# First small-head layer: the transpose that spreads the inverse row sums is issued behind the products with values, not ahead of them

## Chip, cores and metric

The kernel runs on one NeuronCore of one Trainium2 chip. The metric is the device time of one launch in microseconds, the median of three runs. All times inside the profile are from one profiled execution of the same program.

## What is computed

Four pre-norm decoder blocks over x of 8 batches x 128 positions x 256 features, each with an attention-like part, a cross part and a feed-forward part. The change touches only the attention of block 1 ("l1a" in the kernel): 32 query heads of width 8, in 8 groups that share keys and values, causal softmax.

```python
q = (x @ Wq).reshape(B, S, H, dk).transpose(0, 2, 1, 3)      # H = 32, dk = 8
k = (x @ Wk).reshape(B, S, HKV, dk).transpose(0, 2, 1, 3)    # HKV = 8
v = (x @ Wv).reshape(B, S, HKV, dk).transpose(0, 2, 1, 3)
q, k = _rope(q), _rope(k)
qg = q.reshape(B, HKV, G, S, dk)                             # G = 4
scores = jnp.einsum('bhgqd,bhkd->bhgqk', qg, k) / jnp.sqrt(jnp.float32(dk))
attn = jax.nn.softmax(scores + mask, axis=-1)
out = jnp.einsum('bhgqk,bhkd->bhgqd', attn, v)
return out.transpose(...).reshape(B, S, D) @ Wo
```

## The kernel before

Everything is float32 on 128 partitions, in one program with an instruction stream per engine that is written out by hand; semaphores order the engines. PSUM has 8 banks of 512 columns. A plan made ahead gives every job (one filling of a bank) a bank in turn, modulo 8. TensorE's `begin` waits until the bank's earlier user has been read (bank_free), and `end` puts the bank's full signal on the last instruction of the job.

The head loop of l1a works on 64 units (8 batches x 8 key groups). A unit is four heads: 128 queries x 4 x 128 keys of scores, one bank. `heads_plan` makes rounds of three units. In round r the order is: the scores of the round's three units ("s": three matmuls that write the causal mask, then three with the 32 rows of queries and keys), the products with values of a group x of four units where one has become due ("pv"), the transposes of the probabilities of the round before ("t": four 128x128 transposes a unit, twelve a round), and where due the output product of two batches ("o"). There are 16 groups, x = 0 to 15; three rounds of four have one.

The other engines follow the same plan:

- VectorE takes the maxima of each unit's scores (L2425). For pv it first works on the sums of the group (`inverse_of`: L2398, L2400, and L2404, which spreads the 16 inverse sums over 128 columns in SBUF and signals inverse_sums), then copies the unscaled values' products of group x out of the bank (L2445), then scales the outputs of group x - 1 by what the transpose has put into the second half of the same bank (`scaled_outputs`, L2410). It also copies the transposed probabilities of odd units (L2434).
- ScalarE makes the exponentials, four instructions a unit (L1733); the last one frees the bank of the scores. It copies the transposed probabilities of even units (L1739).
- GpSimd folds each unit's probabilities twice (L712, L717) toward the row sums.

So the bank of pv x holds two things: columns 0 to 127 the products of group x with the values, columns 128 to 255 the transposed spread of the inverse sums of group x - 1. The second is one 128x128 transpose, L995, whose source was ready a round before. The products of group x read the copied transposes of units 4x to 4x+3, and wait for the copies of 4x+2 and 4x+3. The inverse of the last group, 15, has a bank of its own ("rb", L1008). Group 0 has no L995.

Lines: L890 is the helper `mm` (all matmuls), L904 the transposes of a normalised input, L987 the transposes of probabilities, L995 the transpose in question.

Of the kernel before, what the change touches and what calls it, by code (L numbers as in the profile page):

```python
# [6 lines left out]
P = 128  # L7
# [237 lines left out]
def build(nc, a, out):  # L245
# [3 lines left out]
    with ExitStack() as ctx:  # L249
# [626 lines left out]
        def _(pe):  # L876
# [74 lines left out]
            def heads(layer, wo, pad):  # L951

                kbd = r3(wk(0, 8 * N), N)
                for key in heads_plan(SUMS_AT if layer == "l2x" else None):
                    if key[0] == "ws":
                        o = begin(layer, "ws")
                        pe.wait_ge(weight_sums, 3)
                        end(mm(o[:, 0:3], cst("ones"), sm(128, 3), True, True))
                        continue
                    if key[0] == "qt":  # L960
                        quantised_transposes("l2x", 0)
                        continue
                    if key[0] == "s":
                        if key[1] % 3:
                            continue
                        units = round_of(key[1] // 3)
                        if layer == "l1a" and UNITS // 2 in units:

                            pe.wait_ge(dve_to_pe.sem, dve_to_pe.next())
                            pe.wait_ge(act_to_pe.sem, act_to_pe.next())  # L970
                        os = [begin(layer, "s", u) for u in units]
                        for u, o in zip(units, os):
                            b = u // 8
                            if pad is None:
                                mm(o, identb[:, :], causalb[:, :], True, False)
                            else:
                                mm(r3(o, P), identb[:, :], pad[:, b * P:(b + 1) * P].unsqueeze(1).to_broadcast([P, 4, P]), True, False)
                        for u, o in zip(units, os):
                            r, b, c = 32 * (u % 4), u // 8, u // 4 % 2
                            end(mm(r3(o, P), XN[r:r + 32, c * N + b * P:c * N + (b + 1) * P],  # L980
                                   kbd[r:r + 32, 4 * c:4 * c + 4, b * P:(b + 1) * P], False, True), layer, "s", u)
                        continue
                    o = begin(layer, *key)
                    if key[0] == "t":
                        pe.wait_ge(*freed(J(layer, "s", key[1])))
                        for i in range(4):
                            ins = nc.tensor.transpose(o[:, i * P:(i + 1) * P],  # L987
                                                      wk(12288 + (key[1] % 8) * G + i * P, P), cst("ident"))
                        end(ins)
                    elif key[0] == "pv":  # L990

                        x = key[1]
                        if layer == "l1a" and x:
                            pe.wait_ge(inverse_sums, x)
                            nc.tensor.transpose(o[:, P:2 * P], inverse_spread(x - 1), cst("ident"))  # L995
                        pe.wait_ge(*freed(J(layer, "t", 4 * x + 2)))
                        pe.wait_ge(*freed(J(layer, "t", 4 * x + 3)))
                        for part in range(1 if layer == "l1a" else 2):
                            for h in range(4):
                                for k in range(4):  # L1000
                                    u = 4 * x + k
                                    window = v_windows[:, u * 32 + 24 - 8 * h:u * 32 + 56 - 8 * h] if part == 0 else ones_window[:, 24 - 8 * h:56 - 8 * h]
                                    ins = mm(o[32 * k:32 * k + 32, part * P:(part + 1) * P], window,
                                             wk(8192 + (u % 8) * G + h * P, P), h == 0, h == 3)
                        end(ins)
                    elif key[0] == "rb":
                        pe.wait_ge(inverse_sums, key[1] + 1)
                        end(nc.tensor.transpose(o[:, P:2 * P], inverse_spread(key[1]), cst("ident")))  # L1008
                    else:
                        bp = key[1]  # L1010
                        for x in range(4):
                            pe.wait_ge(*freed(inverse_job(4 * bp + x) if layer == "l1a" else J(layer, "pv", 4 * bp + x)))
                        for i in range(2):
                            for c in range(2):
                                lo = (bp % 2) * G + (2 * i + c) * P
                                ins = mm(o[:, i * D:(i + 1) * D], XT[:, lo:lo + P],
                                         wo[:, c * D:(c + 1) * D], c == 0, c == 1)
                        end(ins)
# [47 lines left out]
            for b in range(NB + 2):  # L1066
# [6 lines left out]
                if b >= 2:  # L1073
                    x = b - 2
# [1939 lines left out]
```

## Time and profile before

| | us |
|---|---|
| median of three runs | 1522.03 |
| lowest, highest | 1521.43, 1523.54 |
| the profiled execution | 1525.09 |
| its span | 1523.3 |
| head loop of l1a in it, about | 415 to 513 |

The page gives the busy time of each engine over the span: PE (TensorE matmul) 90%, PEld (its weight loads, beside the matmuls) 56%, DVE (VectorE) 60%, ACT (ScalarE) 50%, POOL (GpSimd) 35%. These are averages over some twelve stages with different limits, so a small edit in one stage is read in that stage: in the timeline of each engine, and in the chain of work that ended last. In a timeline row "x12" is twelve instructions merged, and the bracket at the end is the idle time of the engine before them and what the reader of the trace takes for its release. One float32 matmul as written leaves two records (x32 for sixteen), a transpose leaves one. Some matmul records are missing; "x2" for the three mask matmuls is such a place, and the weight loads (x3) show when they began.

### The profile page before, as it was taken

To read this page: it belongs to the slowest core of one execution; us is meant where nothing else is said; L and a number is where in the kernel's file an instruction comes from. 1 tells how busy PE (TensorE), PEld (TensorE's weight loads), DVE (VectorE), ACT (ScalarE), POOL (GpSimd) and SP (SyncE) were. 2 spreads that over 40 slices of the span, in tenths; PEclk is the share of its full clock that TensorE was granted. 3 is DMA by queue.
4 is the path that set the end of the run, shared out by engine and by line. 5 is a ranking of instruction groups with operands and counts; after the bars stand their busy time and mean duration, and the time that the engine had idled before them with its cause. 6 is when DMAs were issued, how large, how long until landed. Compare 5 with 4: busy or idle time off the path is not lost.

```text
span 1523.3 us, 24834 instructions
## 1 busy us (share of the span) xinstructions
PE 1372.9 (90%) x9246; PEld 855.1 (56%) x9264; DVE 919.2 (60%) x1713; ACT 767.3 (50%) x1847; POOL 528.1 (35%) x528
## 2 busy tenths in 40 slices
PE   7869999999888879999999998998996789988799
PEld 3434555565455545666667774664663545545536
DVE  7784322224588755545555788855787587686631
ACT  3452111111788567776776456457776455363230
POOL 3230000000277468886882000110843435414200
PEclk9979999999999999999999999998998798988899
DMA  8020211001200300000000100020001100000100
GB/s 257 26 86 1 68 53 41 1 0 60 107 2 2 126 0 8 8 8 8 8 8 1 77 23 1 1 83 2 2 2 72 56 1 2 3 0 3 30 0 28
DMA packets 21851, 48.06 MB, mean 32 GB/s; under 512 B 1506, under 2 KB 16995, under 8 KB 20580
## 3 DMA queue, kind: packets, MB, share of 16 engines
q1 hardware_dynamic: 21732, 46.47, 8.9%
q8 instruction: 75, 1.23, 0.3%
q14 instruction: 44, 0.36, 0.1%
HBM read 41.22 MB, written 5.24 MB: 31 GB/s over the span
## 4 chain that ended last, share of the span: by engine, by line
PE 64%; DVE 21%; ACT 6%; issue 5%; POOL 4%; DMA 0%; DVEq 0%; ACTq 0%; POOLq 0%
PE PS L890 47%; PE PS L1128 5%; DVE work L2638 4%; PE PS L1187 3%; PE PS L891 3%; ACT work L1733 2%; PE PS L987 2%; PE PS L1225 2%; DVE small L2076 2%; DVE small L2425 1%; PE PS L904 1%; DVE work L2222 1%; DVE X L2617 1%; DVE work L2606 1%; POOL work L823 1%
## 5 line engine op out<-in xcount | busy, mean ns | idle before, releaser
L890 PE MATMUL PS<-XT,WB 128*128 128x512 f32 (+1 forms) x688 | 300.8, 595 | 5.2 <-DVE XT L2102 2.9
L890 PEld LDWEIGHTS PS<-XT,WB 128*128 128x128 f32 (+1 forms) x688 | 127.1, 191 | 149.8 <-issue 146.1
L1733 ACT ACTIVATE work<-PS,small 128x128 f32<-128x128 f32 x512 | 137.7, 416 | 43.6 <-DVE small L2425 43.6
L2297 DVE TENSOR_TENSOR work<-PS,work 128x512 f32<-128x512 f32 x48 | 33.1, 691 | 170.1 <-PE PS L890 170.1
L1659 ACT ACTIVATE work<-PS 128x512 f32<-128x512 f32 x48 | 28.7, 597 | 194.6 <-PE PS L890 194.6
L2425 DVE TENSOR_REDUCE small<-PS 128x4 f32<-128x512 f32 x128 | 80.5, 684 | 36.1 <-PE PS L890 34.6
L890 PE MATMUL PS<-XT,WA 128*128 128x512 f32 (+2 forms) x224 | 97.9, 600 | 4.4 <-DVE XT L2102 2.3
L666 POOL TENSOR_SCALAR small<-small 128x4 f32<-128x4 f32 x22 | 5.1, 230 | 268.3 <-DVE small L2079 268.2
L2638 DVE SCALAR_TENSOR_TENSOR work<-PS,vec,work 128x508 f32<-128x508 f32 (+2 forms) x108 | 80.2, 743 | 13.7 <-DVE work L2638 6.5
L1128 PE MATMUL PS<-WB,work 128*128 128x256 f32 x384 | 86.9, 379 | 0.5 <-DVE work L2302 0.5
L890 PE MATMUL PS<-WA,XT 128*128 128x256 f32 (+1 forms) x384 | 81.5, 374 | 3.6 <-DVE XT L2410 1.8
L1128 PEld LDWEIGHTS PS<-WB,work 128*128 128x128 f32 x384 | 72.8, 190 | 18.3 <-issue 7.7
L890 PE MATMUL PS<-work 128*128 128x64 f32 (+4 forms) x368 | 75.4, 358 | 3.0 <-DVE work L2690 1.8
L890 PEld LDWEIGHTS PS<-WA,XT 128*128 128x128 f32 x384 | 70.7, 202 | 12.8 <-issue 5.0
L701 POOL COPY WB<-WB 128x1536 f32<-128x1536 f32 x8 | 11.7, 1468 | 186.4 <-PE PS L890 186.4
L890 PEld LDWEIGHTS PS<-XT,WA 128*128 128x128 f32 (+2 forms) x224 | 40.0, 189 | 58.2 <-issue 52.1
L1578 ACT ACTIVATE XN<-X,small 128x256 f32<-128x256 f32 x44 | 24.0, 593 | 93.0 <-DVE small L2085 92.9
L987 PE MATMUL PS<-cst,work 128*128 128x128 f32 x512 | 67.2, 281 | 2.7 <-ACT work L1733 2.7
L904 PE MATMUL PS<-cst,XN 128*128 128x128 f32 x176 | 36.0, 353 | 36.3 <-DVE XN L2089 35.5
L890 PE MATMUL PS<-WB,C 128*128 128x256 f32 (+1 forms) x287 | 67.3, 379 | 0.2
L987 PEld LDWEIGHTS PS<-cst,work 128*128 128x128 f32 x512 | 56.3, 143 | 19.4 <-issue 19.4
L1187 PE MATMUL PS<-work 128*128 128x256 f32 x256 | 65.8, 387 | 0.0
(388 smaller groups left out, 2988.3 us busy)
## 6 DMA issues: line engine op xcount, KB each, us to landing
WB<-in_l0f SPq DMA_DIRECT2D x8, 768.0 KB, 8.1
WB<-in_l1x SPq DMA_DIRECT2D x1, 6144.0 KB, 18.3
WB<-in_l0f SPq DMA_DIRECT2D x32, 96.0 KB, 7.2
WB<-in_l2f SPq DMA_DIRECT2D x1, 3072.0 KB, 10.0
WA<-in_l3a SPq DMA_DIRECT2D x1, 2624.0 KB, 9.3
WB<-in_l3f SPq DMA_DIRECT2D x1, 2064.0 KB, 7.9
WA<-in_l1f SPq DMA_DIRECT2D x1, 2056.0 KB, 11.2
C<-in_ctx SPq DMA_DIRECT2D x2, 1024.0 KB, 7.1
```

The costliest lines, as they stand in the source:

```text
L890: mm = lambda o, l, r, s, e: nc.tensor.matmul(o, l, r, start=s, stop=e)
L891: more = lambda o, l, r, e: nc.tensor.matmul(o, l, r, start=False, stop=e, skip_group_check=True)
L904: ins = nc.tensor.transpose(o[:, i * P:(i + 1) * P], source[:, b * D + c * P:b * D + (c + 1) * P], cst("ident"))
L987: ins = nc.tensor.transpose(o[:, i * P:(i + 1) * P], wk(12288 + (key[1] % 8) * G + i * P, P), cst("ident"))
L1128: ins = nc.tensor.matmul(o[:, i * D:(i + 1) * D], l0f_h(x)[:, b * P:(b + 1) * P], quad(x // 3, "down")[:, x % 3 * D:(x % 3 + 1) * D], star ...
L1187: ins = nc.tensor.matmul(o[:, i * D:(i + 1) * D], l1x_q(t // 4, 2 * s_ + i)[:, r * P:(r + 1) * P], wk(8192 + (t // 4 % 2) * 1024 + r * D, ...
L1225: ins = nc.tensor.transpose(o[:, j * P:(j + 1) * P], l1x_p(x)[:, j * D + kc * P:j * D + (kc + 1) * P], cst("ident"))
L1733: f(wk(12288 + (u % 8) * G + h * P, P), bank(j)[:, h * P:(h + 1) * P], ACT.Exp, bias=sm(704 + (u % 8) * 4 + h, 1)).then_inc(*act_step(*([j ...
L2076: v.bn_stats(sm(b * 6, 6), X[:, b * D:(b + 1) * D]).then_inc(*dve_step())
L2297: v.tensor_tensor(l0f_h(m)[:, lo:lo + G], bank(j), l0f_s(m)[:, lo:lo + G], ALU.mult).then_inc(*dve_step(j))
L2425: v.tensor_reduce(sm(704 + (u % 8) * 4, 4), r3(bank(j), P), AX.X, ALU.max, negate=True).then_inc(*dve_step(dve_to_act))
L2638: v.scalar_tensor_tensor(d[:, :, k:P], p[:, :, 0:P - k], vec(taps[0], taps[1] + 3 - k), d[:, :, k:P], ALU.mult, ALU.add).then_inc(*dve_ste ...
```

## The change

The transpose and its wait on inverse_sums go from ahead of the group's two waits and sixteen matmuls to behind them. The bank's full signal is put on the transpose, which is now the job's last instruction; for group 0 it stays on the last product. Nothing else differs.

```diff
                     elif key[0] == "pv":
 
                         x = key[1]
-                        if layer == "l1a" and x:
-                            pe.wait_ge(inverse_sums, x)
-                            nc.tensor.transpose(o[:, P:2 * P], inverse_spread(x - 1), cst("ident"))
                         pe.wait_ge(*freed(J(layer, "t", 4 * x + 2)))
                         pe.wait_ge(*freed(J(layer, "t", 4 * x + 3)))
...
                                             wk(8192 + (u % 8) * G + h * P, P), h == 0, h == 3)
+                        if layer == "l1a" and x:
+                            pe.wait_ge(inverse_sums, x)
+                            ins = nc.tensor.transpose(o[:, P:2 * P], inverse_spread(x - 1), cst("ident"))
                         end(ins)
```

TensorE in a middle round with a group, before: three mask matmuls, three scores, L995, the sixteen products (32x128 outputs), the transposes of the three units of the round before, then the next round's masks. Behind each first instruction stand the semaphores it waits for.

```order
L890 MATMUL PS<-causalb,identb 128x512 [waits bank_free2,bank_free1,bank_free0]
L890 MATMUL PS<-causalb,identb 128x512 x2
L890 MATMUL PS<-work,XN 128x512 x3
L995 MATMUL PS<-cst,work 128x128 [waits inverse_sums,bank_free3]
L890 MATMUL PS<-work,WA 32x128 [waits bank_free7,bank_free6]
L890 MATMUL PS<-work,WA 32x128 x15
L987 MATMUL PS<-cst,work 128x128 [waits bank_free1,bank_free4]
```

The same place in the changed kernel:

```order
L890 MATMUL PS<-causalb,identb 128x512 [waits bank_free2,bank_free1,bank_free0]
L890 MATMUL PS<-causalb,identb 128x512 x2
L890 MATMUL PS<-work,XN 128x512 x3
L890 MATMUL PS<-work,WA 32x128 [waits bank_free7,bank_free6,bank_free3]
L890 MATMUL PS<-work,WA 32x128 x15
L1004 MATMUL PS<-cst,work 128x128 [waits inverse_sums]
L987 MATMUL PS<-cst,work 128x128 [waits bank_free1,bank_free4]
```

The transpose (now L1004) has moved over sixteen products and stands directly ahead of the twelve transposes; the wait for the bank has gone to the first product.

TensorE at the end of the loop, groups 14 and 15, before (the transposes of the last four units stand between the two groups, L1008 and the output product behind the last):

```order
L995 MATMUL PS<-cst,work 128x128 [waits inverse_sums,bank_free5]
L890 MATMUL PS<-work,WA 32x128 [waits bank_free3,bank_free2]
L890 MATMUL PS<-work,WA 32x128 x15
L987 MATMUL PS<-cst,work 128x128 [waits bank_free5,bank_free6]
...
L995 MATMUL PS<-cst,work 128x128 [waits inverse_sums,bank_free2]
L890 MATMUL PS<-work,WA 32x128 [waits bank_free1,bank_free0]
L890 MATMUL PS<-work,WA 32x128 x15
L1008 MATMUL PS<-cst,work 128x128 [waits inverse_sums,bank_free3]
```

And in the changed kernel:

```order
L890 MATMUL PS<-work,WA 32x128 [waits bank_free3,bank_free2,bank_free5]
L890 MATMUL PS<-work,WA 32x128 x15
L1004 MATMUL PS<-cst,work 128x128 [waits inverse_sums]
L987 MATMUL PS<-cst,work 128x128 [waits bank_free5,bank_free6]
...
L890 MATMUL PS<-work,WA 32x128 [waits bank_free1,bank_free0,bank_free2]
L890 MATMUL PS<-work,WA 32x128 x15
L1004 MATMUL PS<-cst,work 128x128 [waits inverse_sums]
L1008 MATMUL PS<-cst,work 128x128 [waits inverse_sums,bank_free3]
```

The order on VectorE, ScalarE, GpSimd and SyncE is the same in both kernels.

## Rows read from the trace of the kernel before

**Rows 1.** The page: length of the span.

```profile
span 1523.3 us, 24834 instructions
```

**Rows 2.** Groups by line and form, 415 to 513 us: busy us, mean ns | idle before.

```profile
L995 PE MATMUL PS<-cst,work 128*128 128x128 f32 x15 | 4.9, 325 | 0.0
```

**Rows 3.** Timeline, 415 to 432 us, ScalarE, weight loads, VectorE: start, us, engine, line.

```profile
420.64 1.17 ACT L1739 ACTIVATE work<-PS 128x512 f32<-128x512 f32 x2
422.56 3.21 ACT L1733 ACTIVATE work<-PS,small 128x128 f32<-128x128 f32 x12 [0.76 <-DVE small L2425]
424.85 0.34 PEld L890 LDWEIGHTS PS<-causalb,identb 128*128 128x128 bf16 x3 [0.54 <-issue]
424.91 0.28 DVE L2445 COPY XT<-PS 128x128 f32<-128x128 f32 x1
```

**Rows 4.** Chain of work that ended last, 502 to 517 us: start, us, what.

```profile
509.39 0.70 DVE work L2434
510.10 0.14 issue
510.23 1.11 PE PS L890 x32
...
511.37 0.30 DVE XT L2445
```

**Rows 5.** Timeline of TensorE's matmuls, groups 0, 1 and the start of 2.

```profile
415.73 1.13 PE L890 MATMUL PS<-work,XN 32*128 32x512 f32 x6
416.80 1.08 PE L890 MATMUL PS<-work,WA 128*32 128x128 f32 x32
...
421.74 0.33 PE L995 MATMUL PS<-cst,work 128*128 128x128 f32 x1
422.00 1.08 PE L890 MATMUL PS<-work,WA 128*32 128x128 f32 x32
423.01 1.53 PE L987 MATMUL PS<-cst,work 128*128 128x128 f32 x12
425.10 0.59 PE L890 MATMUL PS<-causalb,identb 128*128 128x512 bf16 x2 [0.55 <-DVE work L2404]
...
426.94 1.08 PE L890 MATMUL PS<-work,WA 128*32 128x128 f32 x32
```

**Rows 6.** Timeline of TensorE's matmuls at the loop's end, groups 14 and 15.

```profile
505.39 0.33 PE L995 MATMUL PS<-cst,work 128*128 128x128 f32 x1
506.38 1.08 PE L890 MATMUL PS<-work,WA 128*32 128x128 f32 x32 [0.66 <-DVE work L2434]
507.39 1.97 PE L987 MATMUL PS<-cst,work 128*128 128x128 f32 x16
509.19 0.27 PE L995 MATMUL PS<-cst,work 128*128 128x128 f32 x1
510.23 1.08 PE L890 MATMUL PS<-work,WA 128*32 128x128 f32 x32 [0.77 <-DVE work L2434]
```

**Rows 7.** Timeline of all engines, 441 to 456 us, the round of group 5.

```profile
444.16 1.28 DVE L2434 COPY work<-PS 128x512 f32<-128x512 f32 x2
...
445.68 1.08 PE L890 MATMUL PS<-work,WA 128*32 128x128 f32 x32
446.23 3.21 ACT L1733 ACTIVATE work<-PS,small 128x128 f32<-128x128 f32 x12 [1.24 <-DVE small L2425]
...
448.05 1.89 PE L890 MATMUL PS<-WA,XT 128*128 128x256 f32 x8
...
449.57 0.53 PEld L890 LDWEIGHTS PS<-causalb,identb 128*128 128x128 bf16 x3
...
449.98 0.69 DVE L2473 TENSOR_TENSOR X<-PS,X 128x512 f32<-128x512 f32 x1
```

**Rows 8.** Busy time by stretch: PE, PEld, DVE, ACT, POOL; then PEclk, the granted clock.

```profile
515.00:525.00 10.00, 8.00 (x26) 5.22 (x27) 6.19 (x19) 4.95 (x10) 1.27 (x2) 0.83 0.95 314
415.00:513.00 98.00, 86.13 (x936) 55.01 (x952) 84.64 (x181) 75.72 (x258) 68.64 (x119) 1.00 0.01 2
```

## The prediction

> **What bounds the kernel now.** The profiled execution spans 1523.3 us [rows 1]; only 15 instructions are touched, L995, at 0.33 us each and 4.9 us in all [rows 2]. So I read one stage, the head loop of the first small-head layer (about 415 to 513 us of the span), and asked three things: what releases the next round's score products, who waits for the bank with the values, and where a round differs from that pattern.
>
> First the ordinary round. TensorE runs scores, L995, the 32 passes of the products with values (16 matmuls as written, two records each), twelve transposes of probabilities, and then stands still until the next scores. The weight load of those scores starts at 424.85 [rows 3]; ScalarE had begun twelve exponentials at 422.56 that last 3.21 us, so eight of them (two units of the round) end at 422.56 + 8 x 0.2675 = 424.70. The 0.15 left over is what a semaphore takes from one engine to the next; the chain shows 0.14 for it elsewhere [rows 4]. By the plan of banks, units two and three of the next round write where units one and two had their scores. That closes a loop without the products with values: scores, maximum, exponentials of two units, scores. It takes 4.94 us a round (products with values at 422.00 and at 426.94 [rows 5]), and TensorE waits in it. The trace's reader names another releaser for this wait (L2404, a VectorE copy that ended at about the same time) [rows 5], but no semaphore of that copy is among the waits of those matmuls, so I go by the arithmetic.
>
> Second, the readers of the bank. In the round at 421.74 the products are over when the transposes start at 423.01 [rows 5], and VectorE comes to copy the values out (L2445) at 424.91 [rows 3]: some 1.8 us late, since it has maxima and the sums to do first. The bank's being full 0.2 us later is not felt there.
>
> Third, the products themselves wait for the copies of the transposed probabilities, units 4x+2 (ScalarE) and 4x+3 (VectorE), and in the last two rounds only, TensorE's row shows that wait with idle time [rows 6].
>
> **The change part by part.** It removes a transpose ahead of the products and adds it behind, 15 times. Nothing moves on another engine, and no DMA is touched.
>
> *Price of the transpose where it stands.* Ahead of the products it takes 422.00 - 421.74 = 0.26 us of TensorE's time. Without it (round x = 0) the products follow the scores by 416.80 - 415.73 = 1.07 us, as L995 does elsewhere, so the new order has a row for its front [rows 5].
>
> *Price behind.* There it is followed by more 128-row transposes against the same identity. Of sixteen such in a row, 507.39 to 509.19, one takes 1.80 / 16 = 0.11 us, and the seventeenth there is L995 itself [rows 6]. The bounds are 0.11 and 0.26. I take 0.11: same shape, same operand, same neighbour. For TensorE the move is worth 0.26 - 0.11 = 0.15 us a round, if nothing holds the products.
>
> *What holds them.* For x = 1, 4, 7, 10, 13 and x = 3, 6, 9, 12 the copies are done before the scores end (for x = 1 ScalarE's first of two, the one that is needed, from 420.64 on, half of 1.17 [rows 3]); the products start 0.26 earlier and the transposes 0.15 earlier. For x = 2, 5, 8, 11 VectorE's second copy comes last. Shown at x = 5: it ends at 444.16 + 1.28 = 445.44, plus 0.14 is 445.58, where the products start now at 445.68 [rows 7]. They gain 0.10 of the 0.26, since the rest of L995 lay under a wait that remains, and 0.11 is paid behind them: the transposes start 0.01 later. Their end has a margin ahead of the next scores: in the round shown 423.01 + 1.53 = 424.54 against 424.85 [rows 3, 5], so 0.31, and the rounds repeat to 0.02. So the thirteen rounds x = 1 to 13 give **0**: the gain, where there is one, becomes a longer wait for ScalarE.
>
> *The round with an output product* (x = 5, 445 us). Here TensorE does not pause: its output products run from 448.05 up to 449.94 and VectorE's residual add starts at 449.98. The 0.01 of the step above is passed on, no more. The next scores are released by ScalarE's third unit, 446.23 + 3.21 + 0.15 = 449.59, against a weight load at 449.57 [rows 7]. Again **0**, within 0.02; were the full 0.26 paid, it would be 0.16 here. The other output rounds have either no L995 (x between 10 and 11) or wait for VectorE's scaling (x = 12).
>
> *The tail* is where the sign comes from. For x = 14, L995 runs at 505.39 and the products wait until 506.38, 0.66 of it idle, for a VectorE copy [rows 6]. L995 is free there now. Behind the products it stands ahead of the sixteen transposes whose last one feeds the copy at 509.39, which releases the last products at 510.23 [rows 6, 4]: **+0.11**. For x = 15, L995 is again hidden now (0.77 idle after it). Behind the last products it delays the bank's being full, and here VectorE waits for exactly that: products' end 510.23 + 1.11 = 511.34, copy out (L2445) at 511.37, then two scalings, then the output, one chain [rows 4]. The transpose starts 1.01 after the products and takes 0.27 (L995 in a run) to 0.33 (behind other shapes) to be complete [rows 6]; with 0.30 that is 1.31 in place of 1.11, **+0.20**. L1008, the transpose for the last group, comes 0.11 behind it, and the scaling that reads it is the second of the two, so it stays hidden.
>
> Sum: 13 x 0 + 0.11 + 0.20 = **+0.31 us**. Bounds: 0 if both completions overlap fully, and 0.26 + 0.33 + 0.16 = 0.75 if each transpose costs the full price of L995, the round x = 5 among them. The profiled execution took 1525.09 us, 3.06 over the median of 1522.03, of which 1.79 lies around the span; the sum is a difference inside the span and goes onto the median: 1522.03 + 0.31 = **1522.3 us**.
>
> **What a rule of the Trainium skill would make of it.** The row: scores of 32 rows, then a 128-row transpose, then products of 32 columns; the transpose costs 0.26 between two shapes and 0.11 in a run of its own [rows 5, 6]. The rule that bears on it (the Trainium skill, "TensorEngine Tiling (Array Packing)", Key Properties) says that changing the tiling mode, not only the tile, drains the engine. The new order has one such change fewer per round; the trace agrees with 0.15 us. By that rule alone the change would gain, where the sum says that the drain saved lies under ScalarE's exponentials.
>
> **Rivals.** *A, faster: TensorE does set the round.* It is busy 86.13 of 98.00 us in this stage, ahead of VectorE's 84.64 [rows 8], and if the page's releaser were right a round could close elsewhere than I say. Then each of 15 rounds gains 0.15: 1522.0 - 2.2 = 1519.8. Against it: the wait of the next scores ends at 424.85, where the exponentials put it to 0.01. The Trainium skill's rule above is this rival's.
>
> *B, slower: the bank is full later in every round and VectorE feels it.* Place: L2445, in each of 15 rounds. Price: the 0.31 of the last round, 15 x 0.31 = 4.7, so 1526.7. It decides only where VectorE reaches L2445 less than 0.2 us after the products are over; the row has 1.8 us, and only the tail has 0.03.
>
> *C, the clock.* Behind this stage TensorE's granted clock falls to its lower level, 1.2 GHz: 0.83 on average over 515 to 525 us [rows 8], after a pause in which TensorE did nothing. That costs 0.17 x 10 = 1.7 us there. A shift of 0.3 us can move where in the program such a stretch begins or ends. Price: up to 1.7 either way, 1520.6 or 1524.0.
>
> *D, it isn't what it says:* the transpose still runs before the products. The order of the changed kernel excludes it. That the wait on inverse_sums was what L995 hid is excluded too: in none of its 15 places is TensorE's matmul side idle ahead of it (its idle sum is 0.0 [rows 2]), and the "issue" put down to its weight load is the time of the scores.
>
> **How the numbers follow.** My forecast, with its bounds of 0 and 0.75, has 0.80; C 0.10; A 0.05; B 0.03; something not seen 0.02. The three runs lie from 1521.43 to 1523.54, so 0.2% (3.0 us) is about what a measurement can tell from no change, and the forecast, C and A all fall within it. Same 0.93; faster 0.03 (A with a clock gain on top); slower 0.04 (B, or C with the tail's upper bound). The range reaches down to A, 1519.8, and up to 1524.6, which is C's loss, 1524.0, with the tail's upper bound (0.44 over the forecast) and 0.2 for the runs' spread; it leaves out B.
>
> **What would show it.** In the changed profile: L1004 in 15 places, each 0.11 ahead of the first L987 or L1008 behind it; the products 0.26 earlier against the scores in x = 1 and 0.10 in x = 5; the period still 4.94; TensorE's idle before scores longer by up to 0.15; in the tail the copy at L2445 for x = 15 later by 0.3 against the round before. Wrong would be a period other than 4.94 (A if shorter, B if longer), or idle time of VectorE ahead of L2445 in a middle round.

## The result, and the profile after

| | before | after |
|---|---|---|
| runs side by side | 22 | 22 |
| median, us | 1522.82 | 1526.53 |
| lowest, highest, us | 1512.18, 1525.17 | 1520.45, 1530.77 |
| mean and its standard error, us | 1521.94 ± 0.61 | 1525.98 ± 0.57 |
| the profiled execution, us | 1525.09 | 1523.86 |
| its span, us | 1523.3 | 1522.0 |

The ratio after/before is 1.0027 with a 95% interval of 1.0015 to 1.0039: slower by about 4.0 us, where I had given 0.93 to "within 0.2%" and 1524.6 as the upper end. The interval reaches down to +2.3 us, so some of it lies within what I had called the same; its centre doesn't. Two things in the table speak already. Single runs of one kernel lie up to 13 us apart, which the three runs ahead of the prediction (1521.43 to 1523.54) hid. And the one profiled execution of the changed kernel is *shorter* than that of before. So no row of one trace can contain the 4 us; the traces can only show what the edit does locally.

Locally it does nearly what was forecast. The timeline of TensorE's matmuls after, groups 0 and 1 (columns: start, us, engine, line, operation, [idle before <- releaser]), answers to [rows 5]:

```profile
415.12 1.13 PE L890 MATMUL PS<-work,XN 32*128 32x512 f32 x6
416.19 1.08 PE L890 MATMUL PS<-work,WA 128*32 128x128 f32 x32
...
419.55 0.59 PE L890 MATMUL PS<-causalb,identb 128*128 128x512 bf16 x2 [0.81 <-ACT work L1733]
420.07 1.13 PE L890 MATMUL PS<-work,XN 32*128 32x512 f32 x6
421.13 1.08 PE L890 MATMUL PS<-work,WA 128*32 128x128 f32 x32
422.14 0.33 PE L1004 MATMUL PS<-cst,work 128*128 128x128 f32 x1
422.31 1.47 PE L987 MATMUL PS<-cst,work 128*128 128x128 f32 x12
424.49 0.59 PE L890 MATMUL PS<-causalb,identb 128*128 128x512 bf16 x2 [0.71 <-ACT work L1733]
```

The products of group 1 follow their scores by 421.13 - 420.07 = 1.06 us (1.33 before); the transpose, L1004, now stands behind them and delays L987 by 422.31 - 422.14 = 0.17. From mask to mask it is 424.49 - 419.55 = 4.94 us, the period of before. TensorE's idle time ahead of the masks is 0.71 instead of 0.55, and the reader of the trace now names ScalarE's exponentials for it, as the arithmetic had said. The saving of 0.1 to 0.16 a round has become waiting.

The round of group 5, with an output product, answers to [rows 7]:

```profile
443.75 1.13 PE L890 MATMUL PS<-work,XN 32*128 32x512 f32 x6
444.99 1.08 PE L890 MATMUL PS<-work,WA 128*32 128x128 f32 x32
446.00 0.33 PE L1004 MATMUL PS<-cst,work 128*128 128x128 f32 x1
446.17 1.47 PE L987 MATMUL PS<-cst,work 128*128 128x128 f32 x12
447.48 1.89 PE L890 MATMUL PS<-WA,XT 128*128 128x256 f32 x8
449.42 0.59 PE L890 MATMUL PS<-causalb,identb 128*128 128x512 bf16 x2
449.95 0.70 PE L890 MATMUL PS<-work,XN 32*128 32x512 f32 x3
```

And of the same stretch before:

```profile
444.35 1.13 PE L890 MATMUL PS<-work,XN 32*128 32x512 f32 x6
...
446.69 1.53 PE L987 MATMUL PS<-cst,work 128*128 128x128 f32 x12
...
450.52 0.70 PE L890 MATMUL PS<-work,XN 32*128 32x512 f32 x3
```

Products 1.24 behind the scores instead of 1.33 (445.68, [rows 7], less 444.35), transposes 2.42 instead of 2.34, the next scores 6.20 instead of 6.17: 0.03 lost, forecast 0 within 0.02.

The loop's end after, TensorE, answers to [rows 6]:

```profile
505.82 1.08 PE L890 MATMUL PS<-work,WA 128*32 128x128 f32 x32 [1.07 <-DVE work L2434]
506.84 0.33 PE L1004 MATMUL PS<-cst,work 128*128 128x128 f32 x1
507.00 1.91 PE L987 MATMUL PS<-cst,work 128*128 128x128 f32 x16
509.79 1.08 PE L890 MATMUL PS<-work,WA 128*32 128x128 f32 x32 [0.88 <-DVE work L2434]
510.80 0.33 PE L1004 MATMUL PS<-cst,work 128*128 128x128 f32 x1
510.96 0.27 PE L1008 MATMUL PS<-cst,work 128*128 128x128 f32 x1
...
512.32 1.97 PE L890 MATMUL PS<-WA,XT 128*128 128x256 f32 x8 [1.08 <-DVE XT L2410]
```

and VectorE there, the copy of the last group's values, which answers to the last of [rows 4]:

```profile
511.16 0.29 DVE L2445 COPY XT<-PS 128x128 f32<-128x128 f32 x1 [0.38 <-PE PS L1004]
```

From the products of group 14 to those of group 15 it is 3.97 us (3.85 before, [rows 6]); from those to the copy 1.37 (1.14 before). VectorE waits 0.38 for L1004 here and in no other place: of all sixteen copies together the idle time is 0.4, as the groups by line and form (415 to 513 us) say:

```profile
L1004 PE MATMUL PS<-cst,work 128*128 128x128 f32 x15 | 4.9, 328 | 0.0
L2445 DVE COPY XT<-PS 128x128 f32<-128x128 f32 x16 | 4.5, 281 | 0.4 <-PE PS L1004 0.4
```

I measure the loop from the first products (416.80 before, 416.19 after) to the last output product (512.52 and 512.32): **95.72 us before, 96.13 after, +0.41**. It is the measure used for every kernel below ("loop"). The forecast was +0.31. So the edit costs 0.4 us where it stands, and the runs show 4.0. The experiments ask where a factor of ten comes from.

What the page shows of the rest is the granted clock, in 40 slices of about 38 us, 9 for 0.9 or more; after, then before:

```profile
PEclk9979999999999999999999999998998798998989
```
```profile
PEclk9979999999999999999999999998998798988899
```

TensorE falls to its lower level of 1.2 GHz for stretches in some twenty places of the program; some 60% of the clock time lost lies behind 1150 us. A mean clock of 0.953 over 1522.0 us is 0.047 x 1522 = 72 us of clock time lost after, 79 before. The head loop has none in these two traces.

### The profile page after: what moved, and what is told of

It reads as the page before. It is cut to its first block, busy times and chain, and to the rows that moved or that the text cites. A ratio compares the mean times of both kernels' runs of the same rounds, so it can differ in the third digit from the quotient of the medians.

```text
span 1522.0 us, 24819 instructions
## 1 busy us (share of the span) xinstructions
PE 1364.5 (90%) x9246; PEld 851.6 (56%) x9264; DVE 920.0 (60%) x1713; ACT 766.9 (50%) x1847; POOL 531.8 (35%) x528
## 4 chain that ended last, share of the span: by engine, by line
PE 65%; DVE 19%; ACT 7%; issue 4%; POOL 4%; DMA 0%; DVEq 0%; ACTq 0%; POOLq 0%
PE PS L890 48%; PE PS L1128 5%; DVE work L2638 4%; ACT work L1733 3%; PE PS L1187 3%; PE PS L891 3%; PE PS L904 2%; PE PS L1225 2%; PE PS L987 2%; DVE small L2076 1%; DVE small L2425 1%; DVE work L2222 1%; DVE X L2617 1%; DVE work L2606 1%; POOL work L823 1%
## 5 line engine op out<-in xcount | busy, mean ns | idle before, releaser
L890 PE MATMUL PS<-WA,XT 128*128 128x256 f32 (+1 forms) x384 | 78.2, 362 | 4.0 <-DVE XT L2410 2.2
L890 PEld LDWEIGHTS PS<-WA,XT 128*128 128x128 f32 x384 | 67.5, 190 | 13.2 <-issue 5.4
L987 PE MATMUL PS<-cst,work 128*128 128x128 f32 x512 | 66.3, 279 | 2.8 <-ACT work L1733 2.8
L987 PEld LDWEIGHTS PS<-cst,work 128*128 128x128 f32 x512 | 56.9, 143 | 16.8 <-issue 16.8
```

The lines of the kernel that those rows point to most:

```text
L890: mm = lambda o, l, r, s, e: nc.tensor.matmul(o, l, r, start=s, stop=e)
L987: ins = nc.tensor.transpose(o[:, i * P:(i + 1) * P], wk(12288 + (key[1] % 8) * G + i * P, P), cst("ident"))
```

## The experiments

The program's stages are left alone in all but one set; only what stands in the head loop's order, or a short delay, is changed. "Mean" is the mean of all runs of a kernel less the mean of the runs of before on the same chip in the same set, with the standard error of the difference. The first, third and fourth sets below ran on one chip (9), the cut kernels on another (14) and the last set on a third (13); the chip of the first result is not on record. The expectations count the theories in the order in which they came up. The ones that matter: the cost is made by the tail's shift (theory 1) or by the new order in the middle rounds (2); it arises in the loop itself (3); in the stages behind (4); it is a price for each moved transpose or for the place it lands in (5); it comes from TensorE's longer idle time in the rounds (6); the stages behind turn any shift of hundredths into microseconds, by where their low-clock stretches fall (7).

### Which part of the edit costs

Both kernels again, and two mixtures. "Tail only" moves the transpose for groups 14 and 15:

```diff
-                        if layer == "l1a" and x:
+                        if layer == "l1a" and x and not (x >= 14):
...
+                        if layer == "l1a" and x and (x >= 14):
+                            pe.wait_ge(inverse_sums, x)
+                            ins = nc.tensor.transpose(o[:, P:2 * P], inverse_spread(x - 1), cst("ident"))
                         end(ins)
```

"Middle only" has `x < 14` in both places.

> The kernel before, unchanged, beside itself. Every theory expects a ratio of 1.000 with an interval of some 0.002 to each side. What it gives is the scatter of single runs (the earlier runs of this kernel had a standard deviation of 2.9 us) and a second trace, with its total of time at the lower clock.

> The changed kernel, unchanged. If the 3.7 us measured are real they come again: 1.001 to 1.004 of before. If only the 0.4 us seen in the loop of the two traces are real, it is within 0.001 of before. The loop from the first group's products to the output product behind it should take 96.1 us, against 95.7 before, in either case.

> Groups 14 and 15 in the new order, 1 to 13 in the old one. Theory 1: as the changed kernel, 3.7 us over before (1.0024), the loop 96.0 to 96.1 us. Theory 2: 0.4 us over before (1.0003).

> Groups 1 to 13 in the new order, 14 and 15 in the old one. Theory 1 (the local cost is the tail's 0.4 us, and the rest of the 3.7 us is what a stage that ends 0.4 us later does to the clock behind it): no cost, 1.000, and the loop takes 95.7 to 95.8 us. Theory 2 (the new order in the middle rounds costs by itself, in a way that the profiled execution did not show, such as a lower clock in the loop in some runs): 3 us or more over before, 1.002 to 1.003.

| kernel | runs | loop | mean to before | ratio, 95% |
|---|---|---|---|---|
| before again | 12 | 95.68 | -1.4 ± 1.0 | 0.9989, 0.9975 to 1.0003 |
| after again | 12 | 97.71 | +4.7 ± 0.9 | 1.0032, 1.0019 to 1.0045 |
| tail only | 12 | 96.09 | -0.2 ± 0.9 | 0.9996, 0.9982 to 1.0010 |
| middle only | 9 | 95.77 | +4.7 ± 1.0 | 1.0032, 1.0016 to 1.0048 |

The loss repeats: both sets of after together, 34 runs, have a mean of 1526.4. The tail's shift, +0.37 us of loop here, costs nothing that can be told from zero. The middle rounds, whose loop grows by 0.05 us, carry the loss. Theory 1 is gone in the form that the tail's shift makes the loss; theory 2 fits this set.

The trace of after again has one thing that neither recorded trace of the first two had. TensorE at the loop's end:

```profile
503.79 1.08 PE L890 MATMUL PS<-work,WA 128*32 128x128 f32 x32 [1.07 <-DVE work L2434]
504.80 0.39 PE L1004 MATMUL PS<-cst,work 128*128 128x128 f32 x1
504.99 3.55 PE L987 MATMUL PS<-cst,work 128*128 128x128 f32 x16
509.42 1.08 PE L890 MATMUL PS<-work,WA 128*32 128x128 f32 x32 [0.88 <-DVE work L2434]
...
511.94 3.56 PE L890 MATMUL PS<-WA,XT 128*128 128x256 f32 x8 [1.08 <-DVE XT L2410]
```

and by stretch (columns: PE, PEld, DVE, ACT, POOL busy; granted clock; DMA share; GB/s):

```profile
503.00:506.00 3.00, 2.21 (x38) 2.04 (x39) 2.80 (x8) 1.45 (x5) 2.34 (x5) 0.82 0.00 0
506.00:509.00 3.00, 2.54 (x13) 2.20 (x11) 1.11 (x2) 1.20 (x2) 1.92 (x4) 0.61 0.00 0
...
512.00:515.00 3.00, 3.00 (x7) 2.44 (x8) 0.00 (x0) 0.00 (x0) 0.00 (x0) 0.50 0.00 0
```

Sixteen transposes take 3.55 us instead of 1.91, the output product 3.56 instead of 1.97: the clock has gone to 1.2 GHz, after TensorE stood idle 1.07 us where it stood 0.66 before the change. To the end of the output product this loop lasts 511.94 + 3.56 - 414.23 = 101.27 us against 96.13 + 1.97 = 98.10 in the first trace of after: 3.2 us. Of the six traces whose loop ends in the new order two show such a stretch (this one, and "after longer" below), of the fourteen that end in the old order none. The two are among the four traces with the whole edit, where the pause is 1.07 us. In the two that move the tail's transposes alone it is 0.92, because group 13 still runs in the old order, and neither shows the stretch. So tail only does not test it. If it came in half of the executions with the whole edit it would cost 1 to 1.5 us on average, an estimate from four traces. It can be a part of the loss of after. It is not what makes middle only slow, whose pauses there are 0.81 and 0.77 us and whose trace has no such stretch.

### Does it arise in the loop?

Four kernels that end behind the first small-head layer: all later stages are left out, SyncE writes x out where the layer ends, and the sum of four blocks is not computed. VectorE, as an example of the cut:

```diff
+            dve.wait_ge(*dve_last())
+            dve.sem_inc(x_final, 4)
+            return
```

> The kernel before, ended behind the first small-head layer: all stages behind it are left out, and the sum up to there is written out. It is the base of the next three; 517 to 525 us. Theory 3 (the cost arises inside the head loop, as a lower granted clock there in some runs) and theory 4 (it arises in later stages) both expect a narrow scatter here, with the clock at its upper level throughout the loop.

> The changed kernel, cut at the same place. Theory 3: 2 to 5 us over the cut kernel before on average, in runs of two kinds, some 0.4 us over and some 3.5 us or more over with a lower mean clock. Theory 4: 0.4 us over in all runs.

> Groups 1 to 13 in the new order, 14 and 15 in the old, cut at the same place. Theory 3: 2 to 5 us over the cut kernel before, in runs of two kinds. Theory 4: 0.0 to 0.1 us over.

> Groups 14 and 15 in the new order, cut at the same place. Theory 3: 0.4 us over the cut kernel before, no second kind of runs. Theory 4: 0.4 us over as well.

| cut kernel | runs | median | lowest, highest | loop |
|---|---|---|---|---|
| before | 4 | 524.85 | 522.09, 526.15 | 95.86 |
| after | 5 | 524.61 | 523.49, 526.89 | 96.03 |
| middle only | 4 | 524.04 | 520.87, 526.57 | 95.71 |
| tail only | 4 | 522.69 | 520.98, 524.67 | 96.00 |

After less before is +0.7 ± 1.2 us in the mean, middle only -0.6 ± 1.5. With so few runs this excludes 4.4 us for each by about three standard errors, no more; but the loops agree with those of the whole programs. Theory 3 has no support, and with it theory 2; that the loss is made behind the loop is so far what is left, and shown further down. The scatter of 1.6 to 2.3 us is there already: the loop begins between 414.8 and 417.6 us in these four traces, so it comes at least in part from the stages ahead of it, which the edit doesn't touch.

### Which groups?

> Groups 1 to 13 in the new order, again, for nine to twelve more runs and a second trace. If the 4.7 us of the first time are the middle rounds' own, 1.002 to 1.004 again. If they were scatter, within 0.001.

> Only groups 2, 5, 8 and 11 in the new order: those whose products wait for a VectorE copy and gain little. Theory 5 (cost per group, wherever TensorE's idle time or order changes): a share of the 4.7 us by number, 4 of 13, 1.5 us, 1.001. Theory 6 (the cost needs the longer idle time ahead of the scores, which these groups don't get): 0. Theory 7 (no stage has a price: a shift of hundredths of a microsecond tips the clock of later stages, differently in each kernel): any value from -4 to +5 us, with no order among the three kernels of this set.

> Only groups 1, 3, 4, 6, 7, 9, 10, 12 and 13 in the new order: those whose products start at once, so that TensorE's idle time ahead of the next scores grows from 0.55 to 0.71 us. Theory 5: 3.2 us, 1.002. Theory 6: all of the 4.7 us, 1.003. Theory 7: any value.

> The kernel before, with the last transpose of the loop (L1008) issued ten times into the same place, so that the stage ends later by 9 x 0.11 = 1.0 us and nothing in the rounds changes. A plain delay gives 1.0 us, 1.0007. Theory 7 expects another number, between -3 and +6 us, since the later stages then meet the clock differently.

"Held groups" moves the transpose for x = 2, 5, 8, 11 alone, where the products still wait for a copy; "free groups" for the nine others below 14. "Before longer" is before with ten of the last group's transposes in place of one, which writes the same values again and delays the output product:

```diff
-                        end(nc.tensor.transpose(o[:, P:2 * P], inverse_spread(key[1]), cst("ident")))
+                        for _ in range(10):
+                            ins = nc.tensor.transpose(o[:, P:2 * P], inverse_spread(key[1]), cst("ident"))
+                        end(ins)
```

| kernel | runs | loop | mean to before | ratio, 95% |
|---|---|---|---|---|
| middle only again | 12 | 95.75 | +1.7 ± 1.3 | 1.0005, 0.9987 to 1.0023 |
| held groups | 12 | 95.75 | -0.8 ± 1.1 | 0.9998, 0.9980 to 1.0016 |
| free groups | 12 | 95.74 | +5.2 ± 1.1 | 1.0035, 1.0015 to 1.0055 |
| before longer | 12 | 96.35 | +3.8 ± 1.1 | 1.0027, 1.0007 to 1.0047 |

Free groups cost it all, held groups nothing, with loops that are equal to 0.01 us. Middle only is not as slow as in its first set; both together, 21 runs, are at 1525.5. That would fit theory 6: in the free groups TensorE idles longer. But before longer has before's order in every round and costs as much: a loop that is 0.63 us longer at its very end makes 3.8. (I had expected 1.0 us of delay. The ten transposes take 1.28 us instead of 0.30, but TensorE's idle time behind them falls from 0.85 to 0.47.)

### A dose, or not?

> Groups 1, 3, 4, 6, 7, 9, 10, 12 and 13 in the new order, again. If their 5 us are a property of the kernel: 1.002 to 1.005 again. If they were scatter, within 0.001. The head loop should again end within 0.05 us of where it ended before.

> The kernel before, with the transpose issued ahead of the products in all groups as before, and in those nine groups once more behind them (the second writes the same values again). TensorE's idle time ahead of the next scores is then 0.55 - 0.16 = 0.39 us in these rounds, less than before, not more. Theory 6 (longer idle time in the rounds costs, by the clock): no cost, 0.999 to 1.001. Theory 5 (the place of the bank's last instruction costs, whatever the idle time): 5 us, 1.003. Theory 7 (each kernel meets the clock in the later stages in its own way): any value.

> The changed kernel with the last transpose of the loop issued ten times, so that the stage ends about 0.6 to 1.0 us later still. A plain sum of the changed kernel's 4.2 us and this delay, or of this delay's own 3.8 us: 5 to 8 us over before, 1.0035 to 1.005. Theory 7: not additive; anything from -1 to +6 us, and a value at or under the changed kernel's own 4.2 us would speak for it.

> The kernel before with the last transpose of the loop issued seven times: the stage ends about 0.3 us later, which is what the changed order does at the loop's end. Plain delay: 0.3 us, 1.0002. Theory 7 in the form that a later end of the stage by 0.3 to 1 us sets the later stages' clock: 3 us or more, 1.002 and up.

"Free twice" leaves the transpose ahead of the products and issues it once more behind them in the nine free groups, so that TensorE idles less than before (0.44 us ahead of the masks, 0.55 before). "After longer" is after with the ten transposes of before longer; "before little longer" has seven of them.

| kernel | runs | loop | mean to before | ratio, 95% |
|---|---|---|---|---|
| free groups again | 12 | 95.66 | +5.4 ± 1.4 | 1.0042, 1.0023 to 1.0061 |
| free twice | 12 | 95.68 | +2.8 ± 1.4 | 1.0026, 1.0004 to 1.0047 |
| after longer | 12 | 98.11 | +2.2 ± 1.4 | 1.0013, 0.9992 to 1.0034 |
| before little longer | 12 | 95.96 | +5.2 ± 0.8 | 1.0041, 1.0023 to 1.0059 |

Free groups are slower for good: 1527.2 in 24 runs. But there is no dose. A delay of 0.24 us costs 5.2 ± 0.8 and one of 0.63 costs 3.8 ± 1.1, no more, and the delay on top of the whole edit costs 2.2 ± 1.4, no more than the edit alone. A price for each moved transpose (theory 5) can't give that, since the costs of after (4.4) and of the delay (3.8) should add. Free twice, idling less and still 2.8 ± 1.4 above, doesn't decide on theory 6; the two delays, which touch no round, show that longer idle time isn't needed.

### Does a delay cost where nothing stands behind it?

> The kernel before, with the first of the last 128 products of the whole program issued twice, into the same place: 0.44 us more TensorE work on a stretch where TensorE never pauses and behind which there is nothing but the output. Theory 7 (the 4 us come from how later stages meet the granted clock) expects the plain 0.4 us, 1.0003, with the interval over 1.000, since no later stage is left. If any edit of this kernel costs 4 us, whatever stands behind it: 1.002 to 1.004.

> The kernel before, with the two transposes of the router's logits in the feed-forward stage of block 1 (about 830 us into the span) issued three times. Plain delay: 0 to 0.5 us, 1.000 to 1.0003. Theory 7: any value from -3 to +5 us, and whatever it is, the trace shows it arising behind 1050 us, where the clock has its low stretches, not at 830.

The first issues one of the last products of the whole program twice, 0.44 us of TensorE, in the chain that ends last; the last 40 us of the program grow by 0.43 us in its trace. The second issues the router logits' transposes three times, at about 830 us, with the stages behind 1150 us still to come; the stretch around it grows by 0.44 us.

```diff
+                        if bp == 0 and i == 0 and m == 0:
+                            mm(o[:, i * D:(i + 1) * D], wk(m * N + b * P, P), w3("w2", m * D, m * D + D), True, True)
```
```diff
-                for i in range(2):
+                for i in (0, 1) * (3 if layer == "l1f" else 1):
```

| kernel | runs | mean to before | ratio, 95% |
|---|---|---|---|
| delay in the last stage | 12 | -0.2 ± 0.9 | 0.9999, 0.9982 to 1.0015 |
| delay at 830 us | 12 | +1.0 ± 1.2 | 1.0002, 0.9984 to 1.0020 |

So a delay of that size costs nothing that shows when nothing stands behind it, and 4.5 ± 0.7 us (the two delays at the loop's end, 24 runs, less before of their sets) when a thousand microseconds of program do. That is what theory 4 expects, and the part of theory 7 that speaks of the stages behind. One rival stays: this set ran on chip 13, the sets with the slower kernels on chip 9, and no slower kernel was run on chip 13 beside the two delays. That the loss belongs to chip 9 is not excluded. That *any* shift costs is not so: the delay at 830 us, tail only and held groups cost nothing that shows.

### How the stages behind do it

Before again and free groups again happened to give two traces that agree almost throughout: loops of 95.68 and 95.66 us, and at 1150 us, VectorE's timeline, the same instruction (its line moved by the edit) 0.05 us apart (before again, then free groups again):

```profile
1149.81 0.96 DVE L2453 RECIPROCAL work<-PS 128x128 f32<-128x128 f32 x1 [2.16 <-PE PS L890]
```
```profile
1149.76 0.96 DVE L2456 RECIPROCAL work<-PS 128x128 f32<-128x128 f32 x1 [2.16 <-PE PS L890]
```

Then, by stretch (columns as above), before again:

```profile
core 0 of [0], span 1513.5 us
...
1160.00:1180.00 20.00, 11.67 (x55) 5.33 (x55) 15.89 (x28) 12.56 (x21) 11.58 (x11) 0.74 0.06 24
1180.00:1200.00 20.00, 12.87 (x117) 9.61 (x114) 14.73 (x36) 11.86 (x15) 12.82 (x11) 0.83 0.02 4
1240.00:1260.00 20.00, 15.68 (x88) 11.44 (x86) 13.98 (x21) 12.01 (x27) 1.43 (x2) 0.83 0.01 1
```

free groups again:

```profile
core 0 of [0], span 1520.5 us
...
1160.00:1180.00 20.00, 11.68 (x55) 5.40 (x55) 15.88 (x28) 12.54 (x21) 11.62 (x11) 0.74 0.05 21
1180.00:1200.00 20.00, 14.12 (x108) 10.74 (x106) 12.66 (x30) 12.06 (x15) 12.78 (x11) 0.66 0.00 0
1240.00:1260.00 20.00, 16.45 (x73) 12.81 (x73) 13.00 (x19) 11.38 (x18) 0.00 (x0) 0.74 0.01 1
```

From 1160 to 1180 us the rows are the same to a few hundredths. Between 1180 and 1200 one execution is granted 0.83 and the other 0.66, for the same instructions. Both run at the lower clock from 1184 to 1191 us (granted 0.52 and 0.50); from 1191 to 1198 one is back at 1.00 and the other still at 0.53. By 1199 us they are 2.3 us apart, and at the end 7.0. The first had 117 matmuls behind it in those 20 us, the other 108 (roughly, since some records are missing). Behind that, coarser:

```profile
1180.00:1300.00 120.00, 98.12 (x1148) 60.41 (x1147) 83.49 (x155) 58.90 (x105) 53.92 (x51) 0.87 0.05 19
1300.00:1513.00 213.00, 185.97 (x2269) 114.55 (x2267) 119.80 (x272) 70.69 (x135) 44.81 (x48) 0.94 0.04 11
```
```profile
1180.00:1300.00 120.00, 98.06 (x1131) 60.99 (x1129) 81.84 (x150) 59.07 (x105) 52.96 (x51) 0.83 0.05 19
1300.00:1513.00 213.00, 187.47 (x2269) 114.86 (x2265) 121.06 (x277) 70.86 (x135) 45.66 (x49) 0.91 0.03 10
```

0.87 against 0.83 and 0.94 against 0.91: between these two executions the loss is made in the clock, in stages that both kernels have alike.

One pair says nothing yet of the kernels. All sixteen traces of whole programs have the same VectorE instructions in nearly the same order, so the time between two of them can be compared. From the one at 300 us of before's trace to the one at 412 it is 111.7 us in twelve traces and 116.1 in four, which have low-clock stretches from about 376 and 410 us, ahead of the loop. From 412 to 560 it is 147.2 to 147.8 us in fourteen traces, whatever the kernel (147.4 after, 147.7 before), and some 3.5 us more in the two with the stretch in the loop's tail: the 0.4 us of the edit can't be seen any more at 560 us. From 560 to 1180 it is 619.6 to 620.3 in all. Then they part: 115.8 to 120.4 us from 1180 to 1300, and 213.5 to 228.4 from 1300 to 1520. Sorted by what the runs say, in means of the traces:

| stretch of before's trace, us | eight traces of the slower kernels | six of kernels not slower | difference |
|---|---|---|---|
| 0 to 412 | 412.6 | 411.8 | +0.9 ± 1.1 |
| 412 to 1180 | 767.7 | 767.4 | +0.3 ± 0.5 |
| 1180 to 1300 | 118.6 | 118.1 | +0.5 ± 1.0 |
| 1300 to 1520 | 223.4 | 217.5 | +5.9 ± 1.5 |

The slower kernels are those of the next table but before, two traces each; the others are before (twice), tail only, held groups and the two delays of the last set. (One execution a trace: the eight spans are 7.6 us longer in the mean, where the runs say 4 to 5.) So nearly all of the difference between these traces arises behind 1300 us, in stages that no edit but the delay in the last stage touches, and the clock goes with it: of the stretch from 1300 us the slower kernels lose 21.5 us in clock time, the others 15.4.

Every run comes with its mean clock, so this can be asked of all of them, with no trace. Clock time lost is (1 - clock) x span. Before's 146 runs are those of the experiments, whose clocks are on record; after's 34 include the first 22.

| kernels | runs | mean, us | clock time lost, us |
|---|---|---|---|
| before | 146 | 1522.0 ± 0.3 | 70.2 |
| after | 34 | 1526.4 ± 0.5 | 74.6 |
| free groups | 24 | 1527.2 ± 0.7 | 77.6 |
| middle only | 21 | 1525.5 ± 0.8 | 73.6 |
| the two delays at the loop's end | 24 | 1526.4 ± 0.5 | 74.5 |

Tail only, held groups, free twice, after longer and the two delays of the last set have lost 68.7 to 71.4 us.

Over the single runs of each row the time rises by 0.55 to 0.60 us for each microsecond of clock time lost, with a correlation of 0.78 to 0.91. At 0.6, after's 4.4 ± 0.9 us more of lost clock are 2.6 of its 4.4 ± 0.6 us; the loop's 0.4 is at most a small part, and some 1.4 to 1.8 is not accounted for. But the price depends on the place. Over the sixteen traces a microsecond of clock time lost goes with 0.75 us of time between 300 and 412 us, with 0.25 between 513 and 1180, with 0.68 between 1180 and 1300, and with 0.93 behind 1300, where the slower kernels lose theirs. At 0.93 the 4.4 us would be worth 4.1, an estimate that leaves nothing clear of the errors.

The Trainium skill's page "TensorE: Matmul & The Clock Gate" (Part 1, "What's actually happening") calls the behaviour at a ramp run-variable, and says that "the ramp penalty is <1% of a typical kernel span". The traces agree with the first. The second is said of the ramp and is no bound for this kernel, which falls to the lower level again and again: it loses 4.6% of its span in clock time (70 of 1522 us), at 0.6 some 2.8% of its time.

### What stays open

Which kernel's runs come out on which side was not predicted by any theory. Free groups (loop +0.02 or less) and two plain delays (+0.24, +0.63) cost 4 to 5 us; tail only (+0.37) and held groups (+0.03) cost nothing that shows. Whether any of these kernels is slower on another chip than 9 is not shown either. The means of several kernels, tail only, held groups, the delay in the last stage, sit at before's 1522, and those that clearly differ all lie above it. A reading would be that before's runs happen to take a good path through the later stages which some disturbances spoil; no run shows why those and not others. The stretch at the lower clock in the loop's tail (two of the four traces with the whole edit) is a second possible part of after's loss. None of the kernels was faster than before.

## Why the prediction was wrong, point by point

**What bounds the round: right.** ScalarE's exponentials do. The period is 4.94 us after as before, and TensorE's idle time rose from 0.55 to 0.71.

**The price where it stood, 0.26: right** (1.33 to 1.06 in group 1). **The price behind, 0.11: too small.** It is 0.16 to 0.17: a transpose that follows the products' 32 columns isn't one in a run of its own. The nearest row was the wrong one; the value lay between the two bounds I had named, nearer to the lower. It made the held round cost 0.03 instead of 0.01.

**The tail: right in sign, place and mechanism.** +0.12 (forecast 0.11) for group 14 and +0.23 (forecast 0.20) for the last copy, which VectorE waits for in the last group alone. With 0.05 from the rounds ahead the loop is +0.41 (forecast +0.31, bounds 0 and 0.75). The edit that carries this cost alone measures -0.2 ± 0.9.

**Rival A, faster: wrong,** as forecast; the trace agrees with the rule on the tiling mode, since the products start 0.27 earlier against the scores, and the saving is waited away. **Rival B: wrong;** VectorE's copies wait 0.4 us in all, in one place.

**The step that failed is the term for the stages behind,** put at 0 in the sum and priced by rival C, the clock, at 1.7 us either way. I saw that the clock falls behind this stage [rows 8], priced one stretch of it (10 us, 1.7 us) and gave it 0.10. The page's clock row had six slices below 0.9 behind 1140 us and two ahead of it, which I did not add up: 79 us of clock time lost in that execution, some 70 on average, that a shift can rearrange. Its effect is no ±1.7 in one stretch but some 3 us of standard deviation from run to run and 4 to 5 us between kernels. So the sum of local terms, +0.31, was never the term that decides. And the three runs of before, 2.1 us apart, I read as the measure of the scatter; 22 runs spread over 13 us. Why the shift went up and not down stays open.

**A slip that changed nothing:** of the 3.06 us by which the profiled execution of before lay over the median I put 1.79 down to the time around the span. Every execution has that time (1526.32 against a span of 1524.5 in one of after), so it is no part of the 3.06.

With what is known now, the local sum would be 0.4 us and the range some 5 us to either side, with about half of the chance outside "same": of the eleven changed kernels five are clear of before (after, middle only, free groups, the two delays at the loop's end), four show nothing and two are undecided. The direction would still be a guess.

## What to carry to other kernels

Cost an edit locally, by the length of the stage between two instructions that both kernels have, and check it there: that worked here to 0.1 us. Then look at the clock row of everything behind the stage: where TensorE keeps falling to its lower clock, kernels that differ by hundredths of a microsecond can end microseconds apart, and this belongs in the range. To judge an edit of less than 0.5% there, take twenty runs or more of each kernel, compare their mean clock beside their time, and run a plain delay of the same size as a control, on the same chip; one profiled execution can have the opposite sign, as it had here.

## What the hardware showed beyond what was expected

- TensorE fell to 1.2 GHz inside the loop's tail in two of the four traces in which its pauses there were 1.07 and 0.88 us instead of 0.66 and 0.77 (in one of them sixteen transposes took 3.55 us instead of 1.91, 3.2 us in all), and in none of the two with 0.92 and 0.88.
- Two executions 0.05 us apart at 1150 us were granted 0.83 and 0.66 in the same twenty microseconds and ended 7.0 us apart.
- One microsecond of clock time lost goes with 0.6 us of time over whole runs, but with 0.25 to 0.93 by stretch over sixteen traces. That TensorE's work lies under other engines to a different share in each stage would explain it; no run tests that.
- Executions part most behind 1180 us, and little ahead of that: from 560 to 1180 us sixteen traces lie within 0.7 us of each other, from 1300 to 1520 us within 15.
- A lone 128-row transpose costs TensorE 0.26 us between scores of 32 rows and products of 32 columns, 0.16 to 0.17 behind such products and ahead of its like, and 0.11 among its like.
